# The first attention's loop of four batches on each engine, written out step by step with constant places

## The chip, the cores and the metric

The kernel runs on one core of a Trainium2 chip. The time is that of the device for one launch, in microseconds (us), as the median of the runs. The engines are named as in the profile: PE is TensorE (PEld its weight loads), DVE is VectorE, ACT is ScalarE, POOL is GpSimd, SP is the engine that only issues DMAs. Each engine has its own program and its own sequencer; they meet at semaphores.

## The reference

Two layers of cross-attention and a feed-forward part, over 32 batches of 128 tokens of 128 features. The change touches the first attention alone:

```
x = x + tanh(g_xattn[0]) * attention0(layernorm(x), ctx, ctx)   # 16 heads of 8 features
x = x + tanh(g_ffn[0])   * experts0(layernorm(x))
x = x + tanh(g_xattn[1]) * attention1(layernorm(x), ctx)        # 16 heads of 64 features
x = x + tanh(g_ffn[1])   * experts1(layernorm(x))

def attention0(query, key, value):
    Q, K, V = query @ Wq.T + bq, key @ Wk.T + bk, value @ Wv.T + bv   # split into 16 heads
    attn = softmax(einsum('bhqd,bhkd->bhqk', Q, K) / sqrt(8))
    return einsum('bhqk,bhkd->bhqd', attn, V) @ Wo.T + bo
```

## The kernel before

`first_attention` is a pipeline over the 32 batches. In step n each engine does its part of several batches at once: TensorE transposes the normalised tokens of batch n + 4 (L694), projects batch n + 3, spreads the queries and keys of batch n + 2 over the partitions (`stack_up`), makes the scores of batch n + 1 by query (L735), transposes the maxima of batch n (L744), makes the scores of batch n by key (L753, L758), weighs the values of batch n - 1 (L769), and transposes and projects the heads of batch n - 2 (L776, L783, L787). Products that need precision are done as sums of float16 halves by `both_products` (L51). VectorE takes the maxima (L520), copies the maxima (L525) and the heads (L539), makes the low halves (L501, L506), adds the values' bias (L515), adds the result to x (L544) and takes the statistics of batch n + 5 (L495, L315, L497). ScalarE takes the exponentials and copies out of PSUM, GpSimd normalises and splits the context, and from step 8 to 27 also splits a piece of the second attention's weights per step (`split`).

The order on each engine is written by hand, in a function `step(n, s, live)` per engine; what may run when is set by semaphores whose values are counts of batches. `every_step` calls it: steps -5 to 3 are written out with Python numbers, steps 4 to 27 are a loop on the engine itself (`Fori`, rounds 1 to 6, four steps a round), and steps 28 to 34 are written out again. In the loop the batch number is a value in a register, so addresses and semaphore values are computed by small instructions (REGISTER_ALU, ISA) on that engine. `s` is a plain number that only picks buffers and early conditions. GpSimd has its own loop for steps 8 to 27, five rounds of four.

SP issues the loads of tokens and weights, and then eight DMAs of 2178 KB each that clear `expert_rows`, a table in HBM that the second attention fills later; they run beside the first attention.

Of the kernel before, what the change touches and what calls it, by code (L numbers as in the profile page):

```python
# [22 lines left out]
B = 32  # L23
# [18 lines left out]
SPLIT_FROM, SPLIT_TO = 8, 28  # L42
# [332 lines left out]
def normalise(nc, pool, stats, x_b, out, work, s, count):  # L375


    nc.gpsimd.tensor_tensor(work[:, 0:1], stats[:, 1:2], work[:, 3:4], ALU.add).then_inc(s, 1)  # L378
    nc.gpsimd.tensor_tensor(out, x_b, stats[:, 0:1].broadcast_to([P, P]), ALU.subtract).then_inc(s, 1)
    pool.wait_ge(s, count + 2)  # L380
    nc.gpsimd.tensor_tensor(work[:, 1:2], work[:, 0:1], work[:, 2:3], ALU.pow).then_inc(s, 1)
    pool.wait_ge(s, count + 3)
    return nc.gpsimd.tensor_tensor(out, out, work[:, 1:2].broadcast_to([P, P]), ALU.mult)


def first_attention(nc, A, k):
# [12 lines left out]
    R = 4  # L399
    DEEP = 4  # L400
    FIRST, LAST = -5, B + 3
    LOOP = (1, 7)
    with ExitStack() as ctx:
        def sb(name, shape, dt=F32):
            return ctx.enter_context(nc.sbuf_tensor("l0_" + name, shape, dt))
# [35 lines left out]
        def row(t, n):  # L441
            return t[:, bass.ds(n, 1), 0:P].rearrange("p a n -> p (a n)")

        def every_step(engine, step):

            for n in range(FIRST, DEEP * LOOP[0]):
                step(n, n, lambda ahead, n=n: 0 <= n + ahead < B)
            with engine.Fori(*LOOP) as i:
                for s in range(DEEP):
                    step(DEEP * i + s, DEEP * LOOP[0] + s, lambda ahead: True)  # L450
            for n in range(DEEP * LOOP[1], LAST):
                step(n, n, lambda ahead, n=n: 0 <= n + ahead < B)

        def there(n):
            return slice(4 * n, 4 * n + 4)
# [8 lines left out]
        with nc.Block() as block:  # L464
            @block.sync
            def _(sp):
                for n in range(1, LOADS):
                    load_tokens(sp, A, k, n, tokens_landed)
                k.ffn0_total = load_weights(nc, sp, A, k)
                for e in range(E):  # L470
                    sp.dma_start(k.expert_rows[e * REGION:(e + 1) * REGION, :].rearrange("(j p) w -> p j w", p=P),
                                 k.empty_row[:, :].rearrange("p (a w) -> p a w", a=1).broadcast_to([P, REGION // P, ROW])).then_inc(k.rows_cleared, 16)

            @block.vector
            def _(dve):
# [70 lines left out]
                def step(n, s, live):  # L546
# [24 lines left out]
                    if isinstance(n, int):  # L571
# [11 lines left out]
                        if n > B:  # L583
                            k.folded_lo(dve, n - B - 1)

                every_step(dve, step)

            @block.gpsimd
            def _(pool):
                pool.wait_ge(primed, 4)  # L590

                def step(n, s, live):
                    if not live(5):
                        return
                    b, w = n + 5, (s + 5) % 2
                    pool.wait_ge(stats_ready, b + 1)
                    if s + 5 >= 2:
                        pool.wait_ge(T_moved, b - 1)
                    normalise(nc, pool, stats[:, w, :], row(k.x_sb, b), xn[:, w, 0, :], work[:, w, :], norm_step, 3 * b).then_inc(xn_ready, 1)
                    nc.gpsimd.tensor_copy(row(k.cT_hi, b), row(k.ctx_sb, b)).then_inc(cT_hi_ready, 1)  # L600
                    pool.wait_ge(cT_hi_ready, b + 1)
                    nc.gpsimd.tensor_tensor(row(k.cT_lo, b), row(k.ctx_sb, b), row(k.cT_hi, b), ALU.subtract).then_inc(cT_ready, 1)

                    pool.wait_ge(xn_ready, b + 1)
                    if isinstance(b, int) and b == 0:
                        pool.wait_ge(primed, 5)
                    nc.gpsimd.tensor_tensor(taker[:, 1:2], taker[:, 0:1], taker[:, 0:1], ALU.add)
                    nc.gpsimd.tensor_tensor(row(k.x_sb, b), row(k.x_sb, b), bias_row[:, :], ALU.add).then_inc(bias_added, 1)

                def split(c):  # L610
                    some = bass.ds(c * SPLIT_STEP, SPLIT_STEP)
                    nc.gpsimd.tensor_copy(k.w_hi[:, some], k.w_raw[:, some]).then_inc(w_hi_ready, 1)
                    pool.wait_ge(w_hi_ready, c + 1)
                    nc.gpsimd.tensor_tensor(k.w_lo[:, some], k.w_raw[:, some], k.w_hi[:, some], ALU.subtract)

                for n in range(FIRST, SPLIT_FROM):
                    step(n, n, lambda ahead, n=n: 0 <= n + ahead < B)
                pool.wait_ge(k.split_landed, 16 * 4)
                with pool.Fori(SPLIT_FROM // DEEP, SPLIT_TO // DEEP) as i:
                    for s in range(DEEP):  # L620
                        step(DEEP * i + s, DEEP + s, lambda ahead: True)
                        split(DEEP * i + s - SPLIT_FROM)
                for half in range(2):

                    nc.gpsimd.affine_select(out=k.pick_half[:, :, :], in_=k.pick_half[:, :, :], compare_op=ALU.not_equal,
                                            fill=1.0, base=-HD1 * half, pattern=[[-1, H // 2], [0, P]], channel_multiplier=1)\
                        .then_inc(k.picks_ready, 1)
                    pool.wait_ge(k.picks_ready, half + 1)
                pool.wait_ge(k.norms.primed, 2)
                for g in range(4):  # L630
                    k.norms.deviations(pool, g, g % 2, wait=g > 1)

            @block.scalar
            def _(act):
# [27 lines left out]
                def step(n, s, live):  # L662
# [14 lines left out]
                    if live(4):  # L677
                        transposed_hi(n + 4)

                every_step(act, step)  # L680
                for n in range(4):
                    act.wait_ge(k.folded, n // 2 + 1)
# [4 lines left out]
            def _(pe):  # L687
# [145 lines left out]
                for n in range(WARM_UP):  # L833
                    nc.tensor.matmul(sum_bank[:, :], k.pick_strip[:, 0, :], k.pick_strip[:, :, :].rearrange("p j n -> p (j n)"),
                                     start=True, stop=True)
                every_step(pe, step)


# [1147 lines left out]
def build(nc, A, out):  # L1986
    with ExitStack() as ctx:
        k = Setup()
        with ExitStack() as normed:
            with ExitStack() as raw, ExitStack() as banks:  # L1990
                prepare(nc, ctx, normed, raw, A, k)
                k.fold_bank = [banks.enter_context(nc.psum_tensor(f"fold_bank{n}", [P, 512], F32)) for n in range(4)]
                first_attention(nc, A, k)
                first_ffn(nc, A, k, k.norms)
        second_attention(nc, k)
        second_ffn(nc, k, out.rearrange("b t d -> (b t) d"))
# [29 lines left out]
```

## Time and profile before

| | |
|---|---|
| median of 3 runs | 830.37 us (830.29 to 832.22) |
| the profiled execution | 827.14 us |
| its span, first to last instruction | 825.4 us |
| mean granted TensorE clock | 0.988 |
| TensorE busy | 775.6 us, 94% |
| VectorE, ScalarE, GpSimd busy | 76%, 68%, 58% |
| DMA moved | 41.66 MB, 50 GB/s over the span |

The profiled execution is one run under the profiler; its time has some 1.7 us around the span. Times of single instructions are taken from it, the comparison of kernels from the runs. The first attention takes the span from about 11 us to about 207 us.

### The profile page before, as it was taken

Reading aid. Unit: us, or ns where it says so; the run is one execution under the profiler, and the core shown is the slowest. Engines: PE = TensorE matmul, PEld = TensorE weight load, DVE = VectorE, ACT = ScalarE, POOL = GpSimd, SP = SyncE. Lnnn points to the kernel's source line nnn. Section 1 sums busy time; section 2 is a strip of 40 time slices with the busy share of each in tenths; the row PEclk is TensorE's granted clock in tenths of the full one; section 3 lists DMA queues with packets and bytes.
Section 4 is the critical chain, followed back from the end, with each engine's and each line's share of the span. In section 5 each row is a group of like instructions: output and inputs, shape, how many; then the busy total and the mean of one; then the engine's idle time right before and its main releaser. Section 6 shows DMA issues by size and latency. Waiting matters only on the chain. (4 is left out here: it accounts for less than half of the span.)

```text
span 825.4 us, 30718 instructions
## 1 busy us (share of the span) xinstructions
PE 775.6 (94%) x10645; PEld 638.2 (77%) x10647; DVE 626.7 (76%) x2434; ACT 559.3 (68%) x1125; POOL 478.5 (58%) x890
## 2 busy tenths in 40 slices
PE   4999999998999969999999999999999999869995
PEld 2777787776788847888888888888888888538884
DVE  4889999998677765787788788788788787756652
ACT  2678888886455556777777777777777777347772
POOL 6545777772011154676666776666776666526674
PEclk9999999999899998999999999999999999999998
DMA  8999992000200000000000000000000000033010
GB/s 225 348 248 248 230 234 60 0 1 3 71 1 0 0 1 2 2 7 7 3 3 7 7 7 7 3 3 7 7 7 7 1 5 7 14 68 88 27 33 21
DMA packets 61022, 41.66 MB, mean 50 GB/s; under 512 B 8761, under 2 KB 56515, under 8 KB 60720
## 3 DMA queue, kind: packets, MB, share of 16 engines
q1 hardware_dynamic: 57264, 36.39, 17.6%
q0 software_dynamic: 2272, 4.27, 1.6%
q10 hardware_dynamic: 1440, 0.40, 0.3%
q8 instruction: 27, 0.44, 0.2%
q14 instruction: 19, 0.16, 0.1%
HBM read 18.07 MB, written 23.44 MB: 50 GB/s over the span
## 5 line engine op out<-in xcount | busy, mean ns | idle before, releaser
L1597 PE MATMUL l_pv<-l_Z,l_probs 128*128 128x129 f32 x1024 | 164.1, 284 | 0.5 <-DVE l_acc L1149 0.5
L1597 PEld LDWEIGHTS l_pv<-l_Z,l_probs 128*128 128x128 f32 x1024 | 138.4, 191 | 20.1 <-DVE l_acc L1149 9.1
L1382 POOL TENSOR_TENSOR l_qk_lo<-w,l_qk_hi 128x512 f16<-128x512 f32 x132 | 149.1, 1163 | 2.6 <-ACT l_qk_hi L1436 1.8
L1149 DVE SCALAR_TENSOR_TENSOR x_sb<-l_pv,l_inv,x_sb 128x128 f32 (+1 forms) x256 | 89.8, 351 | 35.3 <-DVE l_inv L1136 6.9
L51 PE MATMUL l_tz<-M,cT 128*128 128x512 f16 x396 | 108.0, 382 | 0.0
L1442 ACT ACTIVATE l_probs<-l_b 128x512 f32<-128x512 f32 x128 | 72.8, 594 | 51.7 <-PE l_b L1563 51.7
L1432 ACT ACTIVATE w<-l_qk_bank 128x512 f32<-128x512 f32 x129 | 77.0, 597 | 44.9 <-PE l_qk_bank L51 43.3
L520 DVE TENSOR_REDUCE n_shared<-fold_bank 128x4 f32<-128x512 f32 x128 | 87.3, 683 | 9.5 <-PE fold_bank L735 9.3
L1126 DVE TENSOR_REDUCE l_neg_max<-l_a 128x4 f32<-128x512 f32 x132 | 84.6, 682 | 4.0 <-PE l_a L1541 3.5
L378 POOL TENSOR_TENSOR l_work<-l_stats,l_work 128x1 f32<-128x1 f32 x67 | 12.8, 192 | 124.0 <-DVE l_stats L1101 78.2
L1436 ACT ACTIVATE l_qk_hi<-w 128x512 f16<-128x512 f32 x129 | 80.5, 624 | 1.1
L1447 ACT ACTIVATE l_Z<-l_tz 128x512 f32<-128x512 f32 x128 | 76.7, 599 | 3.9 <-PE l_tz L51 0.2
L1149 DVE SCALAR_TENSOR_TENSOR l_acc<-l_pv,l_inv,l_acc 128x128 f32<-128x128 f32 x224 | 76.6, 342 | 0.0
L365 POOL TENSOR_TENSOR n_rstd<-n_var,n_half 128x4 f32<-128x4 f32 x20 | 20.2, 1009 | 90.0 <-DVE n_var L359 89.9
L51 PE MATMUL l_qk_bank<-cT,w_hi 128*128 (+1 forms) x528 | 55.6, 220 | 3.9 <-PEq L868 2.1
L1136 DVE RECIPROCAL l_inv<-l_pv 128x2 f32<-128x2 f32 x256 | 41.3, 161 | 13.6 <-PE l_pv L1597 13.1
L51 PE MATMUL l_qk_bank<-l_T_hi,w_hi 128*128 128x128 f16 x268 | 49.1, 221 | 1.8 <-DVE l_T_lo L1120 1.8
L51 PEld LDWEIGHTS l_tz<-M,cT 128*128 (+1 forms) x396 | 34.7, 98 | 20.0 <-issue 0.3
L1355 POOL TENSOR_TENSOR l_taker<-l_taker 128x1 f32<-128x1 f32 x97 | 18.0, 193 | 53.2 <-DVE l_slot_i L1208 21.6
L51 PE MATMUL l_qk_bank<-l_T_hi,w_lo 128*128 128x128 f16 x268 | 48.7, 220 | 0.0
L51 PE MATMUL l_qk_bank<-l_T_lo,w_hi 128*128 128x128 f16 x268 | 48.7, 220 | 0.0
L51 PE MATMUL l_qk_bank<-cT,w_lo 128*128 (+1 forms) x264 | 48.2, 220 | 0.0
(282 smaller groups left out, 2288.3 us busy)
## 6 DMA issues: line engine op xcount, KB each, us to landing
expert_rows<-empty_row SPq DMA_DIRECT2D x8, 2178.0 KB, 24.5
x_sb<-expert_rows SPq DMA_DIRECT2D x36, 66.0 KB, 2.2
x_sb<-in_x SPq DMA_DIRECT2D x4, 512.0 KB, 6.9
ctx_sb<-in_ctx SPq DMA_DIRECT2D x4, 512.0 KB, 8.1
w<-in_L_ffn_w SPq DMA_DIRECT2D x1, 2048.0 KB, 9.5
w_raw<-in_L_ffn_gate_w SPq DMA_DIRECT2D x1, 1408.0 KB, 9.1
w_raw<-in_L_ffn_up_w SPq DMA_DIRECT2D x1, 1408.0 KB, 12.0
downT<-in_L_ffn_down_w SPq DMA_DIRECT2D x2, 512.0 KB, 4.1
```

What stands on the lines that cost most here:

```text
L51: last = nc.tensor.matmul(out, lhsT, rhs, start=start and n == 0, stop=stop and n == len(pairs) - 1, skip_group_check=True)
L365: self.nc.gpsimd.tensor_tensor(self.rstd[:, w, :, :], self.var[:, w, :, :], self.half[:, :, :], ALU.pow).then_inc(self.rstd_ready, 1)
L520: nc.vector.tensor_reduce(neg_max[:, s % 2, G * r:G * r + 4], a_bank[r % 2][:, :].rearrange("p (j n) -> p j n", j=4), AX.X, ALU.max, negat ...
L1126: nc.vector.tensor_reduce(neg_max[:, at:at + Q], a_bank[half][:, :].rearrange("p (t n) -> p t n", t=Q), AX.X, ALU.max, negate=True).then_i ...
L1136: nc.vector.reciprocal(inv[:, 2 * m:2 * m + 2], O[:, :, P]).then_inc(inv_ready, 1)
L1149: nc.vector.scalar_tensor_tensor(out=total, in0=O[:, h, 0:P], scalar=inv[:, j:j + 1], in1=total, op0=ALU.mult, op1=ALU.add).then_inc(summe ...
L1382: nc.gpsimd.tensor_tensor(qk_lo[:, w, m, Q * u:Q * u + Q].rearrange("p t n -> p (t n)"), qk[:, u, m, :], qk_hi[:, w, m, Q * u:Q * u + Q].r ...
L1432: nc.scalar.activation(qk[:, u, m, :], qk_bank[:, :], ACT.Copy).then_inc(qk_ready, 1)
L1436: nc.scalar.activation(qk_hi[:, w, m, Q * u:Q * u + Q].rearrange("p t n -> p (t n)"), qk[:, u, m, :], ACT.Copy)\
L1442: nc.scalar.activation(probs[:, at:at + Q, :].rearrange("p h n -> p (h n)"), b_bank[half][:, :], ACT.Exp, scale=float(HD1) ** -0.5).then_i ...
L1447: nc.scalar.activation(Z[:, w, Q * q:Q * q + Q, 0:P], tz_bank[:, :].rearrange("p (h n) -> p h n", h=Q), ACT.Copy)\
L1597: last = nc.tensor.matmul(pv_bank[m % 2][:, h * (P + 1):(h + 1) * (P + 1)], probs[:, 2 * m + h, :], Z[:, w, 2 * m + h, :], start=True, sto ...
```

## The change

`every_step` calls `step` for all steps with Python numbers and has no loop. The last argument, which says whether a batch at some distance exists, is made true for all steps 4 to 27, as it was in the loop, so that the same instructions stand there (batches 32 and beyond, that only pad, included). GpSimd's loop with its `split` is written out in the same way. In the new file lines behind the change have numbers lower by 6 (engines before GpSimd's loop) or 7.

```diff
-    LOOP = (1, 7)
...
         def every_step(engine, step):
 
-            for n in range(FIRST, DEEP * LOOP[0]):
-                step(n, n, lambda ahead, n=n: 0 <= n + ahead < B)
-            with engine.Fori(*LOOP) as i:
-                for s in range(DEEP):
-                    step(DEEP * i + s, DEEP * LOOP[0] + s, lambda ahead: True)
-            for n in range(DEEP * LOOP[1], LAST):
-                step(n, n, lambda ahead, n=n: 0 <= n + ahead < B)
+            for n in range(FIRST, LAST):
+                step(n, n, lambda ahead, n=n: 0 <= n + ahead < B or DEEP <= n < SPLIT_TO)
...
                 pool.wait_ge(k.split_landed, 16 * 4)
-                with pool.Fori(SPLIT_FROM // DEEP, SPLIT_TO // DEEP) as i:
-                    for s in range(DEEP):
-                        step(DEEP * i + s, DEEP + s, lambda ahead: True)
-                        split(DEEP * i + s - SPLIT_FROM)
+                for n in range(SPLIT_FROM, SPLIT_TO):
+                    step(n, n, lambda ahead: True)
+                    split(n - SPLIT_FROM)
```

On TensorE, before, at the end of the loop's body (step 7, 11, ...), these rows stand; behind the branch the epilogue of step 28 begins, with the same row as the body's own head:

```order
L769 MATMUL l_sum_bank<-downT,l_V 32x128 x16
L689 REGISTER_ALU
L691 REGISTER_ALU
L694 MATMUL fold_bank<-ident,n_shared 128x128
L787 MATMUL l_misc<-wo,n_shared 128x128
L448 REGISTER_ALU
L448 COMPARE_AND_BRANCH
L735 MATMUL fold_bank<-l_stack 128x128 x8
```

After the change the same place, the end of step 7 and the head of step 8, reads:

```order
L762 MATMUL l_sum_bank<-downT,l_V 32x128 x16
L687 MATMUL fold_bank<-ident,n_shared 128x128
L780 MATMUL l_misc<-wo,n_shared 128x128
L728 MATMUL fold_bank<-l_stack 128x128 x8
L746 MATMUL l_b<-l_neg_maxT,n_shared 128x128 x8
```

The two register instructions for semaphore values and the two of the loop are gone, and the matmuls stand in the same order (L762 is L769 of before, L780 is L787, L728 is L735, L746 is L753). TensorE's program as a whole grows by the 97 matmuls of a step, twenty times.

On VectorE the loop's end stands at another place of the step, behind the statistics and before the low half of the transposed tokens. Before:

```order
L539 COPY n_shared<-l_misc 128x128
L495 ISA
L495 BN_STATS l_bn<-x_sb 128x6
L314 REGISTER_ALU
L315 COPY l_carrier<-l_carrier 128x1
L497 BN_AGGR l_stats<-l_bn 128x2
L448 REGISTER_ALU
L448 COMPARE_AND_BRANCH
L501 TENSOR_TENSOR l_T_lo<-fold_bank,l_T_hi 128x128
L544 TENSOR_TENSOR x_sb<-l_misc,x_sb 128x128
```

After:

```order
L533 COPY n_shared<-l_misc 128x128
L489 BN_STATS l_bn<-x_sb 128x6
L315 COPY l_carrier<-l_carrier 128x1
L491 BN_AGGR l_stats<-l_bn 128x2
L495 TENSOR_TENSOR l_T_lo<-fold_bank,l_T_hi 128x128
L538 TENSOR_TENSOR x_sb<-l_misc,x_sb 128x128
```

Nothing has moved here either; the register instructions and the branch between L497 and L501 are gone.

## Rows read from the trace of the kernel before

**Rows 1.** The page: busy times, and DMA in 40 slices of 20.6 us.
```profile
PE 775.6 (94%) x10645; PEld 638.2 (77%) x10647; DVE 626.7 (76%) x2434; ACT 559.3 (68%) x1125; POOL 478.5 (58%) x890
...
DMA  8999992000200000000000000000000000033010
```

**Rows 2.** Timeline, weight loads of L744 (steps 11 to 13): start us, duration us.
```profile
87.63 0.14 PEld L744 LDWEIGHTS l_misc<-ident,n_shared 128*128 128x128 f32 x1
...
93.31 0.14 PEld L744 LDWEIGHTS l_misc<-ident,n_shared 128*128 128x128 f32 x1 [0.20 <-DVE x_sb L544]
...
98.69 0.14 PEld L744 LDWEIGHTS l_misc<-ident,n_shared 128*128 128x128 f32 x1
```

**Rows 3.** Window: length, busy us (count) of PE, PEld, DVE, ACT, POOL; PEclk, DMA share.
```profile
93.30:114.90 21.60, 21.08 (x455) 17.18 (x456) 19.79 (x64) 17.71 (x40) 16.14 (x40) 1.00 1.00 231
```

**Rows 4.** Timeline of L744 at steps 3, 4, 5, and of L787 in step 3.
```profile
42.83 0.14 PEld L744 LDWEIGHTS l_misc<-ident,n_shared 128*128 128x128 f32 x1 [0.24 <-DVE x_sb L544]
...
47.17 0.19 PEld L787 LDWEIGHTS l_misc<-wo,n_shared 128*128 128x128 f32 x1 [0.24 <-DVE n_shared L539]
...
48.38 0.14 PEld L744 LDWEIGHTS l_misc<-ident,n_shared 128*128 128x128 f32 x1 [0.32 <-DVE x_sb L544]
...
55.01 0.14 PEld L744 LDWEIGHTS l_misc<-ident,n_shared 128*128 128x128 f32 x1 [0.26 <-DVE x_sb L544]
```

**Rows 5.** Timeline at the turn behind step 11, then behind step 12.
```profile
91.97 0.30 PEld L787 LDWEIGHTS l_misc<-wo,n_shared 128*128 128x128 f32 x2 [0.30 <-DVE n_shared L539]
...
92.54 0.17 PEld L735 LDWEIGHTS fold_bank<-l_stack 32*128 32x128 f16 x6 [0.28 <-issue]
...
92.97 0.29 DVE L544 TENSOR_TENSOR x_sb<-l_misc,x_sb 128x128 f32 x1
...
97.65 0.30 PEld L787 LDWEIGHTS l_misc<-wo,n_shared 128*128 128x128 f32 x2 [0.29 <-DVE n_shared L539]
...
98.07 0.11 PEld L735 LDWEIGHTS fold_bank<-l_stack 32*128 32x128 f16 x4
...
98.36 0.28 DVE L544 TENSOR_TENSOR x_sb<-l_misc,x_sb 128x128 f32 x1
```

**Rows 6.** Waits of TensorE's weight loads, 56 to 200 us: total, times, longest.
```profile
PEld fold_bank L694 <- issue: 4.6, 23, 0.2
...
PEld fold_bank L735 <- issue: 1.5, 5, 0.4
```

**Rows 7.** Instruction queues: 0 to 71.5, 71.5 to 180, 180 to 207 us: packets, MB.
```profile
q8 instruction: 7, 0.11, 0.7%
...
q14 instruction: 1, 0.01, 0.0%
...
q8 instruction: 4, 0.07, 1.1%
```

**Rows 8.** The queue q8 in windows 43.7:44, 50.6:50.8, 62.6:62.8 and 70.7:71.1.
```profile
q8 instruction: 1, 0.02, 23.9%
...
q8 instruction: 1, 0.02, 37.5%
...
q8 instruction: 1, 0.02, 36.1%
...
q8 instruction: 1, 0.02, 18.7%
```

**Rows 9.** Window behind 130 us, columns as in rows 3.
```profile
130.00:135.00 5.00, 4.90 (x114) 4.14 (x113) 4.60 (x16) 4.10 (x10) 3.74 (x10) 1.00 0.05 10
```

**Rows 10.** Timeline in step 4: TensorE's load L694, VectorE's L506.
```profile
53.79 0.14 PEld L694 LDWEIGHTS fold_bank<-ident,n_shared 128*128 128x128 f32 x1 [1.70 <-issue]
...
51.27 0.60 DVE L506 SCALAR_TENSOR_TENSOR l_qk_lo<-fold_bank,bias,l_qk_hi 128x128 f16<-128x128 f32 x2
```

**Rows 11.** Timeline in the last stage; then q8 from 736.6 to 737.0.
```profile
739.85 0.10 PEld L51 LDWEIGHTS f_bank<-w_hi,f_T_hi 128*128 128x128 f16 x1 [1.81 <-issue]
...
q8 instruction: 1, 0.02, 18.8%
```

## The prediction, made before the changed kernel ran

> **What bounds the kernel now.** I read the page first. TensorE is busy for 94% of the span, and DMA stands at eight or nine tenths in the first six slices and at next to nothing behind the seventh [rows 1]. So the part that the change touches runs beside the heaviest transfers of the kernel for its first half, and alone for its second. What the page cannot say is what sets one step of this pipeline. For that I took one line that stands once in every step, the transpose of the maxima at L744, in the timeline: from 93.31 to 98.69 a step takes 5.38 us, and the one before it, from 87.63, takes 5.68 [rows 2]. The longer one is that in which the loop turns round, between steps 11 and 12. In a window of about four steps TensorE works 21.08 of 21.60 us, at its full granted clock, VectorE 19.79 [rows 3]. TensorE has hardly a hole there, so any time in which it gets nothing moves everything behind it by as much, and what the first attention gains or loses should arrive at the end unchanged.
>
> **What register arithmetic costs now.** The loop computes places and semaphore values in registers, and the change takes that away in all 24 looped steps. Does anything wait for it? Step 3 is already written out with constants, step 12 is in the loop. From L744 to the weight load for the heads (L787), through nearly the whole step, TensorE takes 47.17 - 42.83 = 4.34 us in step 3 [rows 4] and 97.65 - 93.31 = 4.34 us in step 12 [rows 2, 5]. So the registers are covered by the work that stands in the engines' queues, and I cost their removal at 0. The bound above is what rounding hides, 0.01 us a step or 0.2 us in all; below it is 0, since fewer instructions can't lengthen this.
>
> **What the loop's turn costs.** Where the loop turns, TensorE's load for the scores (L735) starts 92.54 - 91.97 = 0.57 us after that for the heads (L787); one step later, without a turn, 98.07 - 97.65 = 0.42. That is 0.15 us of branch on TensorE. VectorE has its own turn at another place: its addition L544 starts 1.00 us after the same L787 against 0.71 us, 0.29 later, and the next L744 on TensorE waits for it [rows 2, 5]. That accounts for the 0.30 us by which the step is longer. The loop has six rounds and so five turns, which are also the five waits for "issue" of L735 between 56 and 200 us [rows 6]: 5 x 0.30 = 1.50 us gained. Going into the loop costs less: step 3 takes 48.38 - 42.83 = 5.55 us, 0.17 more than a plain step [rows 4]. Together 1.67 us. ScalarE's and GpSimd's turns lie beside these: they work 17.71 and 16.14 of 21.60 us [rows 3].
>
> **What comes in its place.** The loop's body of four steps stood in the program once and ran six times; now 20 more steps of instructions stand there for every engine, and they have to be brought on chip. The trace has this as DMA queues of their own. Queue q8 carries packets of 16 KB: seven up to 71.5 us, none from there to 180 us (only one of the smaller packets of q14), and four more up to 207 us [rows 7]. That is the picture of a TensorE program whose loop stays where it is once it has been read, and which is read on when the loop is left. In the changed kernel these packets will go on. The last five of the seven start at 43.8 and 50.7, then one between, then at 62.7 and 70.9 us (each window of the group holds one of them) [rows 8]. A packet so lasts TensorE (70.9 - 43.8) / 4 = 6.8 us, or (27.1 - 1.25) / 4 = 6.5 us without the 1.25 us by which step 4 stalled (below). The 109 us from step 8 to the loop's end at 180 us then need 17 more packets, and 58.5 / 6.5 = 9 of them fall before 130 us, while the clearing of expert_rows keeps the DMA engines full: their share is 1.00 in rows 3 and 0.05 behind 130 us [rows 9].
>
> Does such a packet come in time? Step 4 takes 55.01 - 48.38 = 6.63 us, 1.25 more than a plain one [rows 4]. In it TensorE's load L694 starts at 53.79, after 1.70 us in which the profile sees nothing to wait for ("issue") [rows 10], where the same instruction has at most 0.2 us from 56 us on [rows 6]. VectorE's L506, the last work that it needs, had ended at 51.87 [rows 10], and the last packet had started at 50.7, 3.1 us before. The same pair stands at a quite different place: in the last stage TensorE sits idle for 1.81 us of issue up to 739.85, and a packet of q8 started between 736.6 and 737.0, again some 3 us before [rows 11]. I read both as TensorE out of instructions: about 3 us pass from the start of a packet to its first instruction, and in the loaded stretch the start itself can come late. From 62.7 to 70.9 us the spacing is 8.2 us, 1.7 more than the 6.5 that TensorE needs; nothing suffered, because the loop then went back to code that was there. Written out, TensorE would have stood for those 1.7 us.
>
> So of five packets under load two are late, by 1.25 and 1.7 us: 2.95 / 5 = 0.59 us for each. Nine packets: 5.3 us lost. Bounds: nothing, if the two are chance (three of five cost nothing), and 9 x 1.25 = 11.3 us, if each is late as in step 4. I take the mean of the five, as the rows nearest in pace and load. Behind 130 us I cost the packets at 0: up to 200 us no load L694 waits more than 0.2 us for issue [rows 6], though two or three packets came between 180 and 200 us in straight code [rows 7]. If that cover failed, each of the 8 packets there could cost up to the same 1.25 us.
>
> The Trainium skill (Runtime: NRT & Kernel Launch, Instruction fetch mechanics) says that crossing a block of instructions is mostly hidden and that branches are what makes fetches stall, so that unrolling is to be preferred. By that the sum would be the gain of 1.67 us alone. This trace agrees in part: the turns cost something, but the body was not fetched again after 71 us, and a hole of 1.70 us stands inside a step.
>
> The other engines' instructions come in the smaller packets of q14. VectorE issues 64 instructions in four steps where TensorE's two rows have over 900 [rows 3], so a packet lasts it many steps, and I cost its fetches at 0; one late as in step 4 would cost 1.25 us. SP's program and its DMAs are not touched, no wait is added to a queue, and the order of work on every engine stays.
>
> **Sum.** -1.50 - 0.17 + 5.3 = +3.6 us. The profiled execution took 827.14 us with a span of 825.4, and would take 830.7; the median of the runs is 830.37, 3.2 us above the profiled one. Carried over to it: 830.4 + 3.6 = 834.0 us.
>
> **Rivals.**
> *Hidden.* Fetches are in time, since what made the packet of 50.7 us late was the transfers of that moment and not the clearing. For it: the packets up to 62.7 us cost nothing visible. Against: the latest packet of all, at 70.9, lies deep in the clearing. It gives 830.4 - 1.7 = 828.7 us, not to be told from no change. It is also where the skill's rule leads.
> *Faster.* As hidden, and step 4's hole goes as well, because it belongs to the loop's entry and not to the load. For it: the other hole, at 739.85 us, comes when the page shows DMA at three tenths [rows 1]. Against: the entry has its own price one step earlier, and the hole comes almost a step behind it. It gives 830.4 - 1.67 - 1.25 = 827.5 us, 0.35% less. It decides if no packet at all is late.
> *Much slower.* Every packet under load is late as in step 4: -1.67 + 11.3 = +9.6, 840.0 us.
>
> **How the numbers follow.** A measurement of this kernel tells a change from none from about 0.3%, or 2.5 us. The forecast (some packets late, 3 to 8 us of stall in all) has 0.43, much slower 0.08, hidden 0.31, faster 0.18. Of the forecast's 0.43 about 0.08 ends under 2.5 us net and counts as the same. Hence slower 0.43, same 0.39, faster 0.18. As cases of both signs hold most of the chance: the range over all is 828.0 to 840.0 us, and the likeliest case's own is 831.7 to 836.7.
>
> **What would show it.** Steps by L744: none longer by 0.30 us where the turns were (removal right), plain ones still 5.38 (registers cost nothing; shorter ones would prove me wrong there). Queue q8: some 17 packets more between 71 and 180 us. Holes of "issue" before a weight load of TensorE between 71 and 130 us, each some 3 us behind the start of a packet, together 3 to 8 us, and none behind 130. Without holes the forecast is wrong and hidden is right; with holes behind 130 too, it is not the load that makes packets late, and the loss is larger.

## The result, and the profile after

| | before | after |
|---|---|---|
| median | 830.37 us (20 runs, 827.72 to 837.34) | 839.13 us (20 runs, 834.99 to 842.00) |
| ratio of the two | | 1.0096, 95% interval 1.0079 to 1.0112 |
| the profiled execution, its span | 827.14, 825.4 us | 839.59, 837.9 us |
| mean granted TensorE clock | 0.988 | 0.982 |

The kernel is slower by 1.0%, some 8 us by the ratio (the medians are 8.8 us apart). That is the forecast's side and inside its range (828.0 to 840.0), at more than twice the forecast's 3.6 us. The page of the changed kernel, in the lines that answer to [rows 1] and [rows 7] (the queues here over the whole span, where before had 27 packets of q8):

```profile
PE 778.8 (93%) x10647; PEld 639.3 (76%) x10647; DVE 627.4 (75%) x2434; ACT 559.1 (67%) x1125; POOL 477.5 (57%) x890
...
DMA  9999990000200000000000000000000000033010
...
q8 instruction: 45, 0.74, 0.4%
q14 instruction: 24, 0.20, 0.1%
```

TensorE does the same instructions. New are 18 packets of its program, and 5 of the smaller queue q14 (19 before). The first two lines below are q8 from 71 to 130 us and from 130 to 180 us, where before had none; the third is the window 78.4 to 78.7 us, in which one of them starts.

```profile
q8 instruction: 9, 0.15, 1.0%
...
q8 instruction: 8, 0.13, 1.1%
...
q8 instruction: 1, 0.02, 22.6%
```

Next the step's clock, as in [rows 2]: the timeline of the transpose of the maxima, L737 in this kernel, in steps 7 to 10 and 16 to 17 counted as in the prediction (start us, duration us, engine, line).

```profile
64.69 0.14 PEld L737 LDWEIGHTS l_misc<-ident,n_shared 128*128 128x128 f32 x1
...
70.50 0.14 PEld L737 LDWEIGHTS l_misc<-ident,n_shared 128*128 128x128 f32 x1
...
77.40 0.14 PEld L737 LDWEIGHTS l_misc<-ident,n_shared 128*128 128x128 f32 x1
...
86.46 0.14 PEld L737 LDWEIGHTS l_misc<-ident,n_shared 128*128 128x128 f32 x1 [0.53 <-DVE x_sb L538]
...
124.11 0.14 PEld L737 LDWEIGHTS l_misc<-ident,n_shared 128*128 128x128 f32 x1
...
129.50 0.14 PEld L737 LDWEIGHTS l_misc<-ident,n_shared 128*128 128x128 f32 x1 [0.15 <-DVE x_sb L538]
```

Steps 8 and 9 take 77.40 - 70.50 = 6.90 and 9.06 us where step 16, a plain one, takes 129.50 - 124.11 = 5.39. What stands in the long steps is this, the timeline of TensorE's weight loads with the idle time before each in brackets:

```profile
73.19 0.10 PEld L51 LDWEIGHTS fold_bank<-l_T_hi,w0T_hi 128*128 128x128 f16 x1 [1.48 <-POOL cT L596]
...
81.14 0.10 PEld L728 LDWEIGHTS fold_bank<-l_stack 32*128 32x128 f16 x2 [1.93 <-issue]
...
89.12 0.09 PEld L751 LDWEIGHTS l_b<-l_stack 32*128 32x128 f16 x2 [0.70 <-issue]
...
96.69 0.10 PEld L51 LDWEIGHTS fold_bank<-l_qk_lo,stack_sel 128*128 128x128 f16 x1 [1.53 <-issue]
...
109.25 0.15 PEld L762 LDWEIGHTS l_sum_bank<-downT,l_V 128*32 128x32 f32 x7 [0.90 <-issue]
...
117.10 0.11 PEld L728 LDWEIGHTS fold_bank<-l_stack 32*128 32x128 f16 x4 [1.23 <-issue]
...
123.64 0.09 PEld L746 LDWEIGHTS l_b<-l_neg_maxT,n_shared 32*128 32x128 bf16 x2 [0.98 <-issue]
```

The first row names GpSimd, but that operation had ended 0.79 us before TensorE went on, the matmul beside it shows 1.36 us of issue, and in e5 below TensorE passes the same instruction while GpSimd is still at work; it is a hole like the others. The seven stand at different places of a step, so no work of the kernel is what they wait for; packets of q8 start at 70.8, 78.5, 86.5, 94.2, 106.7, 114.2 and 121.4 us, between 2.2 and 2.9 us ahead of them. One more packet of that stretch, at 98.5 us, has no hole behind it. From 124 to 200 us there is none.

The next table adds up, for the profiled execution of every kernel of this study, what the steps take over 5.38 us each, read from the same line of the timeline. It is the key to what follows.

| profiled execution | steps 4-7 | steps 8-15 | steps 16-27 | step 28 |
|---|---|---|---|---|
| before | 1.59 | 0.60 | 0.60 | 0.16 |
| after | 0.99 | 10.58 | 0.00 | 1.09 |
| e1: only TensorE written out | 1.80 | 5.78 | 1.05 | 0.16 |
| e2: all but TensorE written out | 2.55 | 0.51 | 0.51 | 1.06 |
| e3: after, cleared late | 1.84 | 0.01 | 0.00 | 1.06 |
| e4: before, cleared late | 3.17 | 0.61 | 0.59 | 0.16 |
| e5: after, cleared in the feed-forward layer | 1.66 | 0.01 | 0.01 | 1.09 |
| e6: before, the same move | 3.85 | 0.61 | 0.60 | 0.16 |
| e7: after, three cleared early | 0.93 | 4.03 | 0.00 | 1.06 |
| e8: after again | 1.87 | 6.42 | 0.00 | 1.09 |
| e9: before again | 2.65 | 0.61 | 0.59 | 0.16 |
| e10: e5 with the selects earlier | 0.27 | 0.01 | 0.01 | 0.16 |
| e11: TensorE's loop with eight steps a round | 6.63 | 22.29 | 6.18 | 0.16 |
| e12: e10 with the expert biases later | 3.44 | 0.00 | 0.00 | 0.16 |

From before to after that is -0.60 + 9.98 - 0.60 + 0.93 = +9.7, and step 3 gives 0.17 back: +9.5 us, the same as the two timelines have between step 3 and step 31 (152.62 and 162.17 us). The profiled pair is 12.5 us apart; the rest lies behind the attention, and most of it in the last stage (below).

### The profile page after: what moved, and what is told of

The parts are those of the page before. It is cut to its first block and busy times, and to the rows that moved or that the text cites. A ratio compares the mean times of both kernels' runs of the same rounds, so it can differ in the third digit from the quotient of the medians.

```text
span 837.9 us, 30046 instructions
## 1 busy us (share of the span) xinstructions
PE 778.8 (93%) x10647; PEld 639.3 (76%) x10647; DVE 627.4 (75%) x2434; ACT 559.1 (67%) x1125; POOL 477.5 (57%) x890
## 5 line engine op out<-in xcount | busy, mean ns | idle before, releaser
L1119 DVE TENSOR_REDUCE l_neg_max<-l_a 128x4 f32<-128x512 f32 x132 | 84.6, 682 | 4.0 <-PE l_a L1534 3.5
L645 ACT ACTIVATE l_stack<-fold_bank 128x512 f16<-128x512 f32 x64 | 38.9, 608 | 16.9 <-PE fold_bank L51 16.9
## 6 DMA issues: line engine op xcount, KB each, us to landing
w_raw<-in_L_ffn_up_w SPq DMA_DIRECT2D x1, 1408.0 KB, 11.9
```

What stands on the lines that cost most here:

```text
L645: nc.scalar.activation(stack[:, s % DEEP, m].rearrange("p j n -> p (j n)"), stack_bank[:, :], ACT.Copy).then_inc(ready, 1)
L1119: nc.vector.tensor_reduce(neg_max[:, at:at + Q], a_bank[half][:, :].rearrange("p (t n) -> p t n", t=Q), AX.X, ALU.max, negate=True).then_i ...
```

## The experiments

They ran in three groups, e1 to e4, e5 to e8 and e9 to e12, each on a chip of its own. The kernel before took 846.56, 844.83 and 830.11 us in them, so times are compared inside a group only, and profiles of different groups only where steps or holes are compared one by one. In the profiles of the first two groups the last stage stalls in every round of its loop, whatever was edited, and in the third it does not. These are TensorE's waits for issue there in e5, and then in e9 of the third group (total us, times, longest us).

```profile
PEld f_bank L1945 <- issue: 13.2, 13, 1.4
```

```profile
PEld f_bank L1952 <- issue: 1.9, 2, 1.0
```

### e1 and e2: which engine's program it is

```diff
-        def every_step(engine, step):
+        def every_step(engine, step, written_out=False):
+            if written_out:
+                for n in range(FIRST, LAST):
+                    step(n, n, lambda ahead, n=n: 0 <= n + ahead < B or DEEP <= n < SPLIT_TO)
+                return
...
-                every_step(pe, step)
+                every_step(pe, step, written_out=True)
```

e2 is the other way round: VectorE, ScalarE and GpSimd written out, TensorE looped.

> Only TensorE's program is written out; VectorE, ScalarE and GpSimd keep their loops. Theory A (TensorE's instruction packets come late while the clearing fills the DMA engines): nearly the whole loss is here, +6 to +9 us against before, about 45 packets on q8, holes of issue on TensorE between 50 and 126 us and none behind; the turns of VectorE's loop keep about 0.15 us each. Theory B (the other engines' fetches or the loss of their loops cost the time): within 2.5 us of before, and the holes stand elsewhere.

> TensorE keeps its loop; the three other engines are written out. Theory A: 27 packets on q8 as before, no hole of issue on TensorE behind 56 us, the turns shorter (about 0.15 instead of 0.30 us), time -1 to 0 us against before. Theory B: slower by 2.5 us or more, with the holes in VectorE's, ScalarE's or GpSimd's work.

e1 took 850.50 us against 846.56, ratio 1.0050 (1.0028 to 1.0072), with 45 packets of q8 and holes of 1.3 to 1.7 us in front of weight loads at 81.89, 89.18 and 115.13 us. e2 took 847.10, ratio 1.0012 (0.9994 to 1.0030), with 27 packets and no hole behind 54 us. So it is TensorE's program. The size was forecast too high, though: 3.9 us between the medians in e1, where 6 to 9 stood in the expectation. Two things beside that: the turns stay in both (steps of 5.67 us in e1, where TensorE has no loop, and 5.63 in e2, where TensorE alone has one), so the loop of either side alone makes a round longer by nearly as much as both, and the 0.15 us that I gave to TensorE's turn and the 0.29 to VectorE's do not come off one by one; and in e2, not in e1, step 28 is 0.9 us longer, which no theory here had.

### e3 and e4: the load taken from under the attention, in a way that costs more

```diff
                 for e in range(E):
+                    sp.wait_ge(x_done, B)
                     sp.dma_start(k.expert_rows[e * REGION:(e + 1) * REGION, :]...
```

> The changed kernel, but SP starts the eight DMAs that clear expert_rows only when the first attention is done. Theory A (load makes the packets late): the same 45 packets, but no hole of issue from 56 to 200 us, all steps 5.38 us, time -1 to -3 us against before (0.1 to 0.4% faster). Theory C (16 KB of instructions come too late at this pace whatever the load): the holes stay, +6 us or more against before.

> The kernel before (with loops) and the late clearing of the last run. Theory A: the clearing costs the looped kernel nothing, so this is the same as before within 0.2%, turns of 0.30 us still there, and the hole of about 1.25 us in step 4 too, since it comes while the weights are still loaded. If the clearing itself slows the engines, this kernel is faster by more than 0.3% and the gain of the previous run would not be that of the packets.

They took 899.68 and 900.61 us, ratios 1.0638 (1.0611 to 1.0666) and 1.0648 (1.0620 to 1.0676). In e3 all 45 packets came and the steps from 8 to 27 have nothing over 5.38 us. Those are the expected steps; the expected time, 1 to 3 us less than before, is missed by far. The time is lost at one place, in both alike: TensorE's longest waits in e3 from 56 to 270 us begin with

```profile
PEld f_bank L944 <- issue: 55.9, 2, 55.7
```

In e3 SP is at its eight issuing instructions for 54.56 us from 204.37 us on. As I read it, it issues them only as fast as they are carried out (the DMA share from 200 to 250 us is 1.09), and the next stage does not start before SP has left its block. The experiment answers the question of the holes; its time says only that the clearing can't stand there.

### e5, e6, e7, e8: the clearing moved to where nobody waits for it

e5 is the changed kernel with the eight DMAs behind the loads of the first feed-forward layer, e6 the kernel before with the same move, e7 has three where they were and five moved, e8 is the changed kernel itself.

```diff
@@ first_attention, SP
-                for e in range(E):
-                    sp.dma_start(k.expert_rows[e * REGION:(e + 1) * REGION, :]...
@@ first_ffn, SP, behind the loads of downT
+                for e in range(E):
+                    sp.dma_start(k.expert_rows[e * REGION:(e + 1) * REGION, :]...
```

> Written out on every engine as in the changed kernel, but the eight transfers that clear expert_rows are issued in the first feed-forward layer, behind its weight loads, so that they no longer share the DMA engines with the attention. If it is the load that makes TensorE's instruction packets late: some 45 packets of q8, no hole of issue over 0.3 us between 56 and 200 us, every step from 8 on at 5.38 us, and 1 to 3 us less than the kernel before (830 against 832, say; ratio 0.997 to 0.999). If straight code is late with its packets whatever the load: holes of 0.5 to 1.9 us stay between 70 and 125 us and it is 6 to 9 us slower than before, as the changed kernel is. A third way: the clearing now disturbs the feed-forward layer or what comes after, which would show as new waits there in this run and in its looped twin alike.

> The looped kernel with the same move of the clearing. It is the control for the move alone. If the loop has nothing to fetch behind 71 us, the clearing cost the attention nothing there, so the time is that of the kernel before within 0.2%, with the hole of step 4 (1.3 to 2.3 us at 53 us) still there, since the clearing was not yet running then. If the clearing itself slowed the looped attention, this run is faster by over 0.3%; if it costs something in the feed-forward layer, slower by over 0.3%.

> Written out, with three of the eight clearing transfers where they were and five in the feed-forward layer. It is a smaller dose of the load. If the load makes the packets late, the holes of issue end when the third transfer has landed, at about 80 to 90 us, with none behind 95 us, and a third or so of the changed kernel's loss is left (2 to 4 us over the run with all eight moved). If the holes have to do with the place in the code and not with the load, they stay up to 124 us.

> The changed kernel as it is, once more, on the same chip as these three. The ratio to the kernel before should be 1.008 to 1.011 again, the holes of issue stand between 53 and 125 us at nearly the same places of the code, and none behind 126 us. Whether TensorE's granted clock falls to half behind a hole near 81 us is the open point: if the fall belongs to the hole of nearly 2 us, it comes whenever such a hole comes; if it was chance, the clock stays at 1.00 here with holes of the same size.

| | median | against before (844.83) | interval |
|---|---|---|---|
| e5 | 843.37 us | 0.9968 | 0.9944 to 0.9991 |
| e6 | 842.61 us | 0.9967 | 0.9944 to 0.9990 |
| e7 | 845.62 us | 0.9994 | 0.9969 to 1.0019 |
| e8 | 849.42 us | 1.0046 | 1.0025 to 1.0067 |

The waits for issue of TensorE's loads from 71 to 200 us (total us, times, longest us), of e8 and then of e7 and e5:

```profile
PEld fold_bank L687 <- issue: 4.0, 20, 0.2
PEld fold_bank L728 <- issue: 2.8, 2, 1.7
PEld l_b L751 <- issue: 1.8, 1, 1.8
PEld fold_bank L51 <- issue: 1.4, 2, 0.7
```

```profile
PEld fold_bank L687 <- issue: 4.1, 20, 0.4
PEld fold_bank L728 <- issue: 1.6, 1, 1.6
PEld fold_bank L51 <- issue: 0.7, 1, 0.7
```

```profile
PEld fold_bank L684 <- issue: 4.0, 20, 0.2
```

The first line of each is the small regular gap that before has too [rows 6]. The long ones, five by the timeline, are there with eight transfers, two are left with three, none without, though q8 brings the same 18 packets between 71 and 180 us each time. In e7 the last hole ends at 79.51 us, when the third transfer has landed: DMA share 0.29 from 79 to 80 us, 0.02 from 81 to 82. Against e5, e7 costs 2.25 us and e8 6.05: 37% of the loss for three of eight transfers. That settles it: in this kernel straight code on TensorE brings no hole while the DMA engines are free, and costs some 6 us under the clearing. What it is in the load that delays a packet, the engines' time or the memory behind them, these runs do not separate.

e8 is 4.6 us slower than before where the first measurement had 8.8, and its ratio of 1.0046 misses the expected 1.008 to 1.011; the intervals of the ratios don't touch. The two profiled executions of this one kernel lose 10.58 and 6.42 us in steps 8 to 15, so executions differ by some us in how late the packets come, and the chips may too. How much of the difference is which stays open.

e6 was to be the same as before, and is 0.33% faster. Its steps 8 to 27 are those of before, so the attention behind the loads does not account for it, and the kernel before was not profiled in that group. This stays open too.

The clock was the other question. The windows in e7 behind its hole come first, then one of e8 behind a hole of the same length (1.65 us) at the same place of the program. The columns are those of [rows 3], so the granted clock stands behind the five busy times, and the DMA share behind it.

```profile
79.00:80.00 1.00, 0.48 (x16) 0.49 (x18) 0.21 (x1) 0.00 (x0) 0.91 (x1) 1.00 0.29 63
80.00:81.00 1.00, 1.00 (x18) 0.85 (x13) 1.00 (x4) 0.66 (x2) 0.00 (x0) 0.54 0.17 40
81.00:82.00 1.00, 1.00 (x16) 0.74 (x17) 1.00 (x4) 0.91 (x2) 0.00 (x0) 0.50 0.02 4
```

```profile
81.00:82.00 1.00, 1.00 (x25) 0.78 (x19) 1.00 (x4) 0.57 (x2) 0.08 (x1) 1.00 1.24 277
```

e7 fell to half, 1.2 GHz, for 3.4 us, and its step 9 took 8.70 us; e8 stayed at 2.4 GHz and took 7.30. The fall costs 1.4 us, and a hole of this length brings it in one execution and not in another.

### e9, e10, e11, e12: the rest of the account

e10 is e5 with GpSimd's two affine selects on `pick_half`, which stood behind its last split, behind steps 25 and 26. e12 is e10 with the loads of b1 and b2 issued when step 16 is done. e11 is the kernel before with eight steps to a round on TensorE. e9 is the kernel before.

```diff
@@ e10, first_attention, GpSimd
                     split(n - SPLIT_FROM)
+                    if n in (SPLIT_TO - 3, SPLIT_TO - 2):
+                        half = n - (SPLIT_TO - 3)
+                        nc.gpsimd.affine_select(out=k.pick_half[:, :, :], ...
-                for half in range(2):
-                    nc.gpsimd.affine_select(out=k.pick_half[:, :, :], ...
@@ e11, every_step for TensorE
+                with engine.Fori(0, 3) as i:
+                    for s in range(8):
+                        step(8 * i + (s + DEEP), DEEP + s, lambda ahead: True)
@@ e12, first_attention, SP
                 k.ffn0_total = load_weights(nc, sp, A, k)
+                sp.wait_ge(x_done, 16)
+                load_expert_biases(nc, sp, A, k)
```

> The kernel before, profiled on the chip of these three, so that their traces have a looped twin from the same place. Ratio 1.000 within 0.2%; steps of 5.38 us with four or five turns of 5.67, one hole of 1.2 to 2.4 us at step 4, step 28 of 5.54 us, 27 packets of q8. If the last stage there shows holes of issue of about 1.1 us in every round of its loop as the runs of the first two groups do, those belong to the chip or its placement of the program and not to the edits.

> Written out, clearing in the feed-forward layer, and GpSimd's two affine selects on pick_half behind its steps 25 and 26 instead of behind step 27. With every engine but TensorE written out, step 28 had taken 6.44 to 6.47 us instead of 5.54, since VectorE's small additions L357 or L359 lasted 1.07 to 1.10 us instead of 0.17 while the second select ran. If a select that has started holds such an addition until its end: step 28 takes 5.4 to 5.6 us, L357 and L359 0.15 to 0.17 us each, and the kernel is 0.9 us shorter than with the clearing moved alone. If that longer step has another cause (an instruction packet of VectorE, say): it stays at 6.4 us. Against the kernel before: ratio 0.995 to 0.998.

> The kernel before, but TensorE's loop has a body of eight steps and three rounds. If a body stays on chip as long as it fits: 3 to 5 packets of q8 more than before's 27, holes of issue under the clearing up to about 100 us at most, none behind, and a time 1 to 4 us over the kernel before. If a body of eight is too long to stay: some 45 packets as in the kernel written out, holes up to 124 us, and 4 to 8 us over. If nothing is ever kept and only a body of four happens to be covered: packets all the way, as in the second case.

> As the run with the selects moved, and in addition the loads of the expert biases b1 and b2, which land as thousands of very small packets between 47 and 55 us, are issued when step 16 is done (about 135 us). If it is these that make TensorE's packet at 50 us late: the hole of 1.2 to 2.4 us at 53 to 55 us goes, step 4 takes 5.4 us, and the kernel is 1.3 us shorter. If it is the large weights that land in that time: the hole stays. If small packets disturb a fetch wherever they are: a hole of about 1 us moves to 137 us or so.

| | median | against before (830.11) | interval |
|---|---|---|---|
| e9 | 829.65 us | 0.9997 | 0.9975 to 1.0018 |
| e10 | 827.98 us | 0.9964 | 0.9946 to 0.9982 |
| e11 | 857.26 us | 1.0309 | 1.0272 to 1.0347 |
| e12 | 828.88 us | 0.9961 | 0.9938 to 0.9983 |

**The select.** In the changed kernel VectorE's timeline in step 28, and GpSimd's beside it (two selects of 1.1 us in one row, the second from 193.72 us):

```profile
193.74 1.10 DVE L357 TENSOR_SCALAR n_var<-n_stats 128x2 f32<-128x2 f32 x1
194.75 0.15 DVE L359 TENSOR_SCALAR n_var<-n_stats 128x2 f32<-128x2 f32 x1
...
192.49 2.32 POOL L618 TENSOR_SCALAR_AFFINE_SELECT pick_half<-pick_half 128x1024 bf16<-128x1024 bf16 x2
```

The same lines in e10:

```profile
183.99 0.17 DVE L357 TENSOR_SCALAR n_var<-n_stats 128x2 f32<-128x2 f32 x1
184.07 0.16 DVE L359 TENSOR_SCALAR n_var<-n_stats 128x2 f32<-128x2 f32 x1
```

An addition of two columns lasts until the select ends that began 0.02 us before it. In before L357 began at 185.34 and the second select at 185.56 us, behind it, and nothing was held. (The first select ended there at about 185.41 us, between the starts of the two additions, and neither was longer than 0.17.) GpSimd written out reaches the second select some 0.2 us earlier against VectorE, and what is gone between its operations is the register instructions; in e2 it is L359 that is caught, in 1.07 us. With the selects elsewhere step 28 is back at 5.54 us. The Trainium skill (SBUF — State Buffer, Who interferes with whom) has it that the two engines share one pair of ports, that whichever starts first keeps it for its whole instruction, and that a `tensor_scalar` is among the operations that can take it. These rows agree: 1.10 and 1.07 us against 0.17 and 0.16.

**The loop of eight.** The timeline of TensorE where the two turns of e11 are, and q8 from 71 to 180 us:

```profile
113.71 0.23 PEld L743 LDWEIGHTS fold_bank<-l_stack 32*128 32x128 f16 x5 [8.13 <-issue]
...
167.65 0.13 PEld L743 LDWEIGHTS fold_bank<-l_stack 32*128 32x128 f16 x4 [3.72 <-issue]
...
q8 instruction: 17, 0.28, 1.1%
```

So a body of four steps is read once and kept, and one of eight, as far as the count of packets tells, is read anew in each round: 49 packets over the span, more than written out. And where the loop turns the engine stands for 8.13 us under the clearing and 3.72 us behind it. At the first turn the packets of q8 start at 99.5, 107.4 and 110.7 us and the work at 113.71: what is at the head of the body seems not to be asked for before the jump. The Trainium skill says this of turns (Runtime: NRT & Kernel Launch, Instruction fetch mechanics): a jump to a target that isn't among the pages on chip waits for its fetch. The 8.13 and 3.72 us agree.

The kernel loses 27 us, where I had given this case 4 to 8. I had counted late packets and neither the turns, 11.9 us together, nor the clock: in the profile TensorE stood again and again, and its granted clock was 0.85 over this stretch, where one hole in the changed kernel had brought it down for 3.4 us alone.

```profile
56.00:173.00 117.00, 94.82 (x1787) 77.40 (x1788) 79.08 (x248) 70.06 (x157) 58.33 (x149) 0.85 0.77 155
```

**The hole at step 4.** It is in most executions, looped or not, but of every length. TensorE's longest wait for issue from 52 to 57 us in e9 and in e12:

```profile
PEld fold_bank L694 <- issue: 2.5, 1, 2.5
```

```profile
PEld fold_bank L730 <- issue: 1.5, 1, 1.5
```

e10's profile has none of it, and e12's has it though the small packets of the biases were gone. So it isn't these alone, against what I had expected, and e10 escaped it in that one execution; its cause among the large loads was not tried further.

## Why the prediction was right in direction and wrong in size

- *Registers cost nothing*: right. Plain steps are 5.38 us written out as they were looped.
- *The turns cost 0.30 us each, the way in 0.17*: right for four of the five and for the way in. Steps 16 to 27 go from 0.60 over to 0.00, step 3 from 5.55 to 5.38 us. But step 7, where the first turn is, takes 5.72 us in before and still 5.65 in e10, where nothing is late; that turn gives back 0.07, and what else makes step 7 longer I did not find.
- *Some 17 more packets between 71 and 180 us, nine of them under the clearing*: right as a count, 9 up to 130 us and 8 behind. But the one at 70.8 us, just ahead of them, has its hole in step 8, and those at 125.6 and 129.9 have none: the packets that matter are the eight from 70.8 to 121.4 us.
- *About 3 us from a packet's start to its first instruction, holes of issue under load and none behind*: right, 2.2 to 2.9 us, and e5, e7 and e3 show that it is the load. By the rule of the Trainium skill (Runtime: NRT & Kernel Launch, Instruction fetch mechanics) that the prediction weighed, crossing a block is mostly hidden; e5 agrees, with 18 packets and no hole, and the changed kernel does not.
- *The mean of the five packets, 9 x 0.59 = 5.3 us*: this is the step that failed in size. In the profiled execution steps 8 to 15 lose 10.58 us, 1.32 for each of the eight packets; in e8 they lose 6.42, in e1 5.78 with two turns in it. What was wrong is how many are late, not by how much: seven of the eight have a hole, 8.75 us together or 1.25 each, where the mean counted two late ones in five, with 1.25 and 1.7. In e8 it is five holes of 0.66 to 1.77 us. The five packets of before were not like those behind them. With the DMA engines free (e5) the last two of the same five start at 60.6 and 66.4 us; under the clearing they start at 62.6 and 70.8 us (62.7 and 70.9 in before), 2 and 4.4 us later. From the hole of step 4 up to there TensorE stands in none of these kernels; behind the packet of 70.8 us the holes begin. In e7 the packet that follows its last hole starts at 80.6 us, only 3.8 us behind the one of 76.8, and with the load gone there is no further hole. I read this as a lead of the fetches over the work: the delay of the early packets used it up, and so they looked harmless, and the later ones no longer had it. No run tests that reading by itself.
- *The clock*: the sum had no term for it. Of the 10.58 us some 1.5 are the clock, a term that the sum did not have: it fell to half from 81.2 to 84.6 us, and step 9 took 9.06 us where e8's took 7.30 with a hole 0.28 us shorter. The windows of after from 80 to 84 us:

```profile
80.00:81.00 1.00, 0.00 (x0) 0.00 (x0) 0.00 (x0) 0.00 (x0) 0.92 (x2) 1.00 1.23 279
81.00:82.00 1.00, 0.85 (x18) 0.86 (x18) 0.54 (x1) 0.00 (x0) 0.30 (x1) 0.59 1.21 269
82.00:83.00 1.00, 1.00 (x14) 0.80 (x11) 1.00 (x5) 0.66 (x2) 0.00 (x0) 0.50 1.25 234
83.00:84.00 1.00, 1.00 (x16) 0.74 (x17) 0.94 (x3) 0.92 (x2) 0.00 (x0) 0.50 1.25 237
```

- *VectorE, ScalarE and GpSimd change nothing*: wrong by 0.93 us. Their fetches are indeed free (e2), but GpSimd runs ahead by some 0.2 us and its select meets VectorE's addition.
- *Packets behind 130 us cost nothing*: right. (Of before's four packets behind 180 us all had started by 199.2 us; "two or three" before 200 is a miscount, and changes nothing.)
- *"What the first attention gains or loses should arrive at the end unchanged"*: right for what the change does. In the profiled pair 2.7 us were added in the last stage, between its start (L243, at 725.20 and 735.01 us) and the end. There the clock fell for 6.8 us in after, not at all in before, and for 3.4 us when the same kernel was profiled again as e9, so this belongs to the execution and not to the change. From L243 to the end the stage takes 102.9 us in after, 100.2 in before and 101.8 in e9. The windows of after, of before and of e9 at that place, with the clock again behind the five busy times:

```profile
745.00:750.00 5.00, 3.96 (x21) 3.29 (x21) 1.91 (x6) 2.00 (x6) 0.00 (x0) 0.68 0.26 61
```

```profile
735.00:740.00 5.00, 2.92 (x22) 2.36 (x22) 2.93 (x13) 3.21 (x8) 0.00 (x0) 1.00 0.30 68
```

```profile
735.00:740.00 5.00, 4.29 (x21) 3.45 (x21) 1.82 (x6) 1.68 (x5) 0.00 (x0) 0.66 0.28 62
```

Put together from the runs, writing out costs -1.20 for four turns, -0.07 for the first, -0.17 for the way in, +0.93 for the select, and +6.42 (e8) to +10.58 us (the first profile) for the packets: +5.9 to +10.1 us. The hole of step 4 is left out, as it differs from execution to execution of one kernel. Measured as medians are +4.6 in the group of e8 and +8.8 in the first measurement.

## What to carry to other kernels

In this kernel a loop in the busiest engine's program was worth what it saved in fetches: before unrolling, look at the queue that brings that engine's instructions, and at what the DMA engines do meanwhile; if they are full, either keep a body that stays on chip or move the bulk transfer to where nobody waits for it (e10 is 0.36% faster than before that way, and e6, looped, 0.33%, so the writing out itself has no measurable share in it). The body that didn't stay, e11, was worse than both. And an edit on an engine with slack still moves its instructions against those of others: after it, look for short operations that have become long.

## What was not expected of the hardware

- A loop's body of four steps stays with TensorE for 109 us without a packet; one of eight is fetched in each round, and its turns cost 8.13 and 3.72 us, against 0.30.
- A VectorE addition of 128x2 took 1.10 us when a GpSimd select had begun 0.02 us before it.
- TensorE's granted clock fell to 1.2 GHz for 3.4 us behind a hole of 1.65 us in one execution and not in another, at the same place in the program, and cost 1.4 us.
- SP took 54.56 us to issue eight clearing DMAs of 2178 KB in e3, and TensorE stood for 55.7 us beside it, between two stages.
